# Attention and mixture of experts in one program: barriers between the stages removed, PSUM banks dealt anew, the gating moved into the last sequence, the attention's drain between the first experts

## The chip, the cores and the metric

The kernel runs on one core of one Trainium2 chip. The metric is the device time of a run in microseconds; lower is better. TensorE is called PE here, VectorE DVE, ScalarE ACT, GpSimd POOL and SyncE SP, as in the profile.

## What is computed

`x` has 16 sequences of 256 tokens of width 128, all in fp32. Four layers follow each other, each added to `x`:

```python
x = x + attn_a(layernorm(x))   # 16 heads of 8, q and k rms-normed, softmax, projection with bias
x = x + ffn(layernorm(x))      # 8 experts, the best two per token, and one shared expert
x = x + attn_b(layernorm(x))   # differential attention, 16 half-heads, rotary, projection
x = x + ffn(layernorm(x))      # the same weights again
```

In `ffn` every token gets softmax scores over 8 experts, keeps the best two, and the token times its score goes through `silu(xe @ w1[e]) * (xe @ w3[e]) @ w2[e]`; the shared expert takes the unscaled token.

## The kernel before, in words

All of `x` stays in SBUF. The attention layers (`attention_a` and `attention_b`) work on one sequence at a time, the feed-forward layers (`feed_forward`, called twice, with tags f and h) on chunks of 512 tokens (two pairs of tiles, i.e. two sequences), eight chunks in all. Each layer gives one `body` for each of PE, ACT, POOL and DVE, and a body emits the instructions of one step for its engine. All order is written out by hand: an engine runs its queue strictly in the order in which the bodies emit, and semaphores (class `Events`) tie the engines together.

A step of an attention is one sequence, cut into 16 slots h. `AT_A` and `AT_B` say at which slot each task runs, `STAGE_A` and `STAGE_B` for which sequence it does so: projection and normalisation run up to three or four sequences ahead of the scores, the output part one behind. In a step the PE makes the scores (L301 in A, L726 in B), ACT their exponentials (L414, L890), the PE the products with the values (L315, L756), which are copied out (L578 on DVE in A, L897 on ACT in B). One step later come the transposes of the output (L353, L820), the tokens' scaling on DVE (L545 and L548; L1053 to L1060), transposes (L360, L828), a copy (L439, L945), the output projection (L366, L834), the residual and the statistics for the next layer norm (L556 to L571, L1077 to L1097). B also has row maxima: the PE computes scores into two banks (L743) and DVE reduces them (L1023), eight times a sequence, two sequences ahead; and in its output part a difference, a square, a power and a product on POOL (L970 to L986), with a mean on DVE between them (L1066).

A step k of a feed-forward is one chunk, cut into nine slots e, one per expert and one for the shared one. At slot e the PE makes `up` of the next expert (six matmuls, L1211 to L1213, since each fp32 product is made from a high and a low part), the spread of the scores of an expert three ahead (L1207) and `down` of this one (L1241, eight matmuls by the profile). DVE scales (L1387), ACT makes the high part (L1320), POOL or DVE the low part (L1351, L1392), ACT the silu (L1305), DVE the product (L1403). Between them stands the gating of the next chunk: normalise (L1412), `x_turn` (L1258), copy (L1339), `logits` (L1264), `best` (L1421 to L1442), exponentials (L1328 on ACT for the first chunk, L1361 on POOL else), `gates` (L1448 to L1461), `s_turn` (L1271), copy (L1331). `FF` says at which slot each runs. Step -1 makes the gating and the first expert's `up` for chunk 0.

The program is one block for the setup and then four blocks: A with the step -1 of f behind it, f with the first two steps of B's preparation beside its last chunk (`BESIDE`), B with the step -1 of h, and h. Between blocks all engines meet at a barrier. `attention_steps` runs the 16 sequences (step 15 as a whole) and then step 16, the drain, slot by slot; at the slots of `SLOT_AT` it puts in the nine slots of the feed-forward's step -1:

```python
    slot = 0
    for h in range(HEADS):
        body(Step(None, 0, NSEQ), NSEQ, (h,))
        while slot <= E and SLOT_AT[slot] == h:
            following(Step(None, 0, -1), -1, (slot,))
            slot += 1
```

`feed_forward_steps` runs chunks 0 to 7 and a ninth step for the last residual. In PSUM (eight banks of 512 columns) A has scores in banks 0 to 3, the values' product in 4, the k and q transposes in 5, x and qkv in 6, the output part in 7; the feed-forward has its gating in 0, the spread in 1, H1 in 2 and 3, H3 in 4 and 5, Y in 6 and 7; B has x and qkv in 0, transposes in 1, maxima in 2 and 3, scores in 4 and 5, the values' product in 6 and the output part in 7.

Of the kernel before, what the change touches and what calls it, by code (L numbers as in the profile page):

```python
# [225 lines left out]
def attention_a(nc, ctx, g, psum):  # L226
# [401 lines left out]
    layer.ex_sb, layer.qkv_sb, layer.ot_sb, layer.rstd_sb = ex_sb, qkv_sb, ot_sb, rstd_sb  # L628
# [21 lines left out]
def attention_b(nc, ctx, g, psum, before):  # L650
# [26 lines left out]
    XB, QK, PV, OB = bank(0), bank(1), bank(6)[:, 0:SEQ], bank(7)  # L677
    M, S = psum[:, 1024:2048], psum[:, 2048:3072]
# [24 lines left out]
    def tensor(pe):  # L703
# [8 lines left out]
        def body(n, k, part=range(HEADS)):  # L712
# [34 lines left out]
            def values(m, km, q):  # L747

                if q == 0:
                    pe.wait_ge(v_sb.sem, v_sb.upto(m))  # L750
# [257 lines left out]
    def vector(dve):  # L1008

        def body(n, k, part=range(HEADS)):  # L1010
# [115 lines left out]
    layer.ex_sb, layer.qkv_sb, layer.qf_sb, layer.mx_sb, layer.ot_sb = ex_sb, qkv_sb, qf_sb, mx_sb, ot_sb  # L1126
    layer.rstd_sb = rstd_sb
# [6 lines left out]
SLOT_AT = (0, 2, 3, 6, 9, 9, 12, 14, 15)  # L1134
# [4 lines left out]
}  # L1139


def feed_forward(nc, ctx, g, tag, psum, before, out=None):
# [53 lines left out]
    def tensor(pe):  # L1196
        def body(n, k, part=range(E + 1)):
            run, gate = 0 <= k < NCH, 0 <= k + 1 < NCH

            def spread(m, km, e):  # L1200
# [73 lines left out]
            for e in part:  # L1274
# [5 lines left out]
                if gate and e == FF["x_turn"]:  # L1280
                    x_turn()
                if gate and e == FF["logits"]:
                    logits()
                if gate and e == FF["s_turn"]:
# [9 lines left out]
    def scalar(act):  # L1294
        def body(n, k, part=range(E + 1)):
            run, gate = 0 <= k < NCH, 0 <= k + 1 < NCH

# [24 lines left out]
            for e in part:  # L1322
                for m, km, next_e in ahead(n, k, e, 1):
                    silu(m, km, next_e)
                if k == -1 and e == FF["best"]:
# [3 lines left out]
                if gate and e == FF["st_sb"]:  # L1329
# [4 lines left out]
                if gate and e == FF["xt_sb"]:  # L1334
# [39 lines left out]
    def vector(dve):  # L1374
        def body(n, k, part=range(E + 1)):
            run, gate = 0 <= k < NCH, 0 <= k + 1 < NCH

# [105 lines left out]
            for e in part:  # L1483
# [11 lines left out]
                if gate and e == FF["best"]:  # L1495
                    best()
                if gate and e == FF["gates"]:
# [17 lines left out]
    layer.st_sb, layer.xe_sb, layer.h_sb, layer.rstd_sb = st_sb, xe_sb, h_sb, rstd_sb  # L1515
# [3 lines left out]
def attention_steps(eng, body, first, following):  # L1519
# [7 lines left out]
    for n in range(12, NSEQ):  # L1527
        body(Step(None, 0, n), n)
    slot = 0
    for h in range(HEADS):  # L1530
        body(Step(None, 0, NSEQ), NSEQ, (h,))
        while slot <= E and SLOT_AT[slot] == h:
            following(Step(None, 0, -1), -1, (slot,))
            slot += 1


def feed_forward_steps(eng, body, following=None):


    for n in (0, 1):  # L1540
        body(Step(None, 0, n), n)
# [10 lines left out]
    body(Step(None, 0, 8), 8)  # L1552

# [161 lines left out]
```

## Time and profile before

| | |
|---|---|
| Median of 3 runs | 1043.95 us (1042.01 to 1045.37) |
| The profiled execution: its time | 1042.84 us |
| its span, first to last instruction | 1041.0 us |
| PE busy | 885.7 us (85%), 7264 matmuls |
| DVE busy | 728.2 us (70%) |
| ACT busy | 579.5 us (56%) |
| POOL busy | 524.1 us (50%) |
| mean granted clock of the PE | 0.957 |

A busy time is the time in which an engine executes; what is idle is a wait or nothing to do. The page also cuts the span into 40 equal slices and gives the clock granted to the PE in each. Views of the trace give the same for any stretch, and the instructions of an engine in order of time, merged where the same line repeats, with the idle time before them and who ended it.

### The profile page before, as it was taken

The numbers are of one execution on the slowest core, as the hardware profiler recorded it, in microseconds if no ns is written. First come the engines' busy times: TensorE is split into PE (matmuls) and PEld (weight loads), VectorE is DVE, ScalarE is ACT, GpSimd is POOL, SyncE is SP. The second block draws the span as 40 slices with busy tenths as digits, with TensorE's granted clock in tenths as the row PEclk, the third lists the DMA queues.
The fourth block names the chain that finished last, engine by engine and source line by source line (L and its number), as shares of the span: only waits on it lengthen the run. The fifth ranks groups of instructions, "written<-read, shape, count | busy, mean of one in ns | idle before, by whom it ended". The sixth has DMA issues, their size and how long they took to land. (4 is left out here: it accounts for less than half of the span.)

```text
span 1041.0 us, 22276 instructions
## 1 busy us (share of the span) xinstructions
PE 885.7 (85%) x7264; PEld 628.1 (60%) x7264; DVE 728.2 (70%) x1970; ACT 579.5 (56%) x905; POOL 524.1 (50%) x606
## 2 busy tenths in 40 slices
PE   0498988887699999998788988888878499999998
PEld 0245555544478777886555555555544388888887
DVE  4357777775467777775568989899882477777775
ACT  1177777767344444443368888888875244444443
POOL 2556666674145455552425757575642354444441
PEclk9999999999699999999869999999996699999999
DMA  8000000000000000000000000000000000000000
GB/s 223 0 2 2 0 0 0 0 2 2 0 1 1 1 1 1 0 1 1 0 1 2 2 0 0 0 0 0 1 1 1 1 1 11 12 12 10 10 11 21
DMA packets 14591, 8.70 MB, mean 8 GB/s; under 512 B 1600, under 2 KB 14144, under 8 KB 14528
## 3 DMA queue, kind: packets, MB, share of 16 engines
q1 hardware_dynamic: 12944, 7.28, 2.5%
q8 instruction: 35, 0.57, 0.2%
q10 hardware_dynamic: 1584, 0.62, 0.2%
q14 instruction: 28, 0.23, 0.1%
HBM read 5.80 MB, written 2.10 MB: 8 GB/s over the span
## 5 line engine op out<-in xcount | busy, mean ns | idle before, releaser
L1320 ACT ACTIVATE f_xe_hi<-f_xe 128x512 fp32r<-128x512 f32 x128 | 80.9, 632 | 201.9 <-DVE f_xe L1387 201.9
L1023 DVE TENSOR_REDUCE s_qs<-psum 128x4 fp32r<-128x1024 f32 x128 | 156.4, 1222 | 43.7 <-PE psum L743 43.0
L1351 POOL TENSOR_TENSOR f_xe_lo<-f_xe,f_xe_hi 128x512 fp32r<-128x512 f32 x64 | 83.6, 1306 | 189.4 <-ACT f_xe_hi L1320 189.4
L1241 PEld LDWEIGHTS psum<-w,f_h 128*128 128x128 f32 x1152 | 148.5, 192 | 8.8
L1241 PE MATMUL psum<-w,f_h 128*128 128x128 f32 x1152 | 153.8, 277 | 0.0
L414 ACT ACTIVATE s_probs<-psum 128x1024 f32<-128x1024 f32 x128 | 125.5, 1024 | 31.8 <-PE psum L301 31.5
L890 ACT ACTIVATE s_probs<-psum 128x1024 f32<-128x1024 f32 x128 | 131.2, 1025 | 19.4 <-PE psum L726 17.8
L1211 PE MATMUL psum<-f_xe_hi,w_hi 128*128 128x512 f32 x288 | 127.7, 444 | 11.7 <-POOL f_xe_lo L1351 7.3
L1403 DVE TENSOR_TENSOR f_h<-psum,f_g 128x512 f32<-128x512 f32 x144 | 99.1, 688 | 49.0 <-ACT f_g L1305 35.5
L1213 PE MATMUL psum<-f_xe_lo,w_hi 128*128 128x512 f32 x288 | 114.9, 399 | 0.0
L1212 PE MATMUL psum<-f_xe_hi,w_lo 128*128 128x512 f32 x288 | 114.3, 397 | 0.0
L1387 DVE TENSOR_TENSOR f_xe<-psum,f_xt 128x512 f32<-128x512 f32 x128 | 87.3, 682 | 29.2 <-PE psum L1207 29.2
L1305 ACT ACTIVATE f_g<-psum 128x512 f32<-128x512 f32 x144 | 84.7, 588 | 23.9 <-PE psum L1213 23.6
L1361 POOL TENSOR_TENSOR f_p<-euler,f_sh 128x8 f32<-128x8 f32 x56 | 90.1, 1637 | 1.8
L726 PE MATMUL psum<-s_qt,s_kt 32*128 32x256 f32 x512 | 67.1, 339 | 22.1 <-DVE s_qs L1023 15.0
L726 PEld LDWEIGHTS psum<-s_qt,s_kt 32*128 32x128 f32 x512 | 40.7, 192 | 65.3 <-DVE s_qs L1023 30.4
L1392 DVE TENSOR_TENSOR f_xe_lo<-f_xe,f_xe_hi 128x512 fp32r<-128x512 f32 x64 | 44.3, 692 | 44.7 <-ACT f_xe_hi L1320 42.8
L743 PE MATMUL psum<-s_kt,s_qp 24*128 24x256 f32 x512 | 67.4, 342 | 9.0 <-PEq L1634 4.8
L756 PE MATMUL psum<-s_probs,s_v 128*32 128x256 f32 x1024 | 72.4, 402 | 0.0
L1211 PEld LDWEIGHTS psum<-f_xe_hi,w_hi 128*128 128x128 f32 x288 | 54.7, 190 | 28.9 <-issue 9.0
L315 PE MATMUL psum<-s_probs,s_v 128*32 128x256 f32 x1024 | 70.2, 393 | 0.0
L578 DVE COPY s_ot<-psum 128x256 f32<-128x256 f32 x64 | 26.8, 419 | 54.4 <-PE psum L315 54.3
(179 smaller groups left out, 1761.2 us busy)
## 6 DMA issues: line engine op xcount, KB each, us to landing
x<-in_x SPq DMA_DIRECT2D x4, 512.0 KB, 9.9
out<-x SPq DMA_DIRECT2D x8, 256.0 KB, 2.3
w<-in_w SPq DMA_DIRECT2D x3, 512.0 KB, 6.9
select_raw<-in_select SPq DMA_DIRECT2D x1, 512.0 KB, 5.0
rope_cos<-in_rope_cos SPq DMA_DIRECT2D x1, 256.0 KB, 3.6
rope_sin<-in_rope_sin SPq DMA_DIRECT2D x1, 256.0 KB, 4.5
wqkv_a<-in_Wqkv_aT ACTq DMA_DIRECT2D x1, 192.0 KB, 6.0
bqkv<-in_bqkv ACTq DMA_DIRECT2D x1, 192.0 KB, 7.1
```

The lines of the kernel that those rows point to most:

```text
L414: act.activation(dst, src, ACT.Exp).then_inc(ex_sb.sem, 1)
L726: ins = pe.matmul(S[:, o:o + SEQ], kt[r:r + 32, k % 2, q, c * P:(c + 1) * P], qt[r:r + 32, k % 2, q, :], start=True, stop=True)
L890: act.activation(probs[:, 2 * (i % 4):2 * (i % 4) + 2, :, :].rearrange("p j c s -> p (j c s)"), S, ACT.Exp).then_inc(ex_sb.sem, 1)
L1023: dve.tensor_reduce(o[:, r:r + 2, 2 * p:2 * p + 2, 24:25].bitcast(F32R), M.rearrange("p (r j s) -> p r j s", r=2, j=2), AX.X, ALU.max, neg ...
L1211: pe.matmul(dst, w_hi, x_hi, start=True, stop=False)
L1212: pe.matmul(dst, w_lo, x_hi, start=False, stop=False)
L1213: return pe.matmul(dst, w_hi, x_lo, start=False, stop=True)
L1241: ins = pe.matmul(Y[k % 2][:, t * P:(t + 1) * P], g.f_h[:, q, t * P:(t + 1) * P], g.w2[:, e, :], start=(e == 0 and t == 0), stop=(e == NE ...
L1305: act.activation(g.f_g[:, q, :], H1[q], ACT.Silu).then_inc(g_sb.sem, 1)
L1361: pool.tensor_tensor(g.f_p[:, i * w:(i + 1) * w], g.euler[:, 0:w], g.f_sh[:, i * w:(i + 1) * w], ALU.pow).then_inc(pw_sb.sem, 1)
L1387: dve.tensor_tensor(xe[:, e % 2, :], SB, xt[:, km % 2, :], ALU.mult).then_inc(xe_sb.sem, 1)
L1403: dve.tensor_tensor(g.f_h[:, q, :], H3[q], g.f_g[:, q, :], ALU.mult).then_inc(h_sb.sem, 1)
```

## The change

1. The four blocks become one: every engine runs `all_steps`, A, f, B and h in a row, with no barrier between them. SP's stores of the output stand in the same block.
2. The banks: B has scores in 2 and 3, maxima in 0 and 1, the values' product in 4, transposes in 5, x and qkv in 6, the output part in 7. The feed-forward has H1 in 0 and 1, H3 in 2 and 3, Y in 4 and 7, the spread in 5, the gating in 6. So gating and spread share their banks with the attention's preparation and not with its scores.
3. Step 15 of an attention is now emitted slot by slot too, and slots 0 to 7 of the feed-forward's step -1 stand in it, at the slots of `LEAD`. Within that step, `FF_LEAD` takes the place of `FF`.
4. In the drain (step 16) stand slot 8 of step -1 and all nine slots of chunk 0, at the slots of `TAIL_A` or `TAIL_B`; `feed_forward_steps` begins with chunk 1.
5. What the barriers assured is now assured by waits: for the last exponentials, for the last copy out of the values' bank, for the last residual, for the last transposes' use, and for the statistics of the layer before.

```diff
@@ attention_b, PE: values and o_turn
+                if km == 0 and q == 0:
+                    pe.wait_ge(before.x_sb.sem, before.x_sb.upto(Step(None, 0, NCH - 2)))
...
+                if km == 0 and c == 0:
+                    pe.wait_ge(before.x_sb.sem, before.x_sb.upto(Step(None, 0, NCH - 1)))
@@ attention_b, DVE: normalise
+                if km == 4:
+
+                    dve.wait_ge(before.rstd_sb.sem, before.rstd_sb.upto(Step(None, 0, NCH - 1)))
@@
-SLOT_AT = (0, 2, 3, 6, 9, 9, 12, 14, 15)
+LEAD = {1: (0,), 3: (1,), 4: (2,), 6: (3,), 8: (4,), 9: (5,), 13: (6,), 15: (7,)}
+TAIL_A = {1: ((-1, 8),), 4: ((0, 0),), 8: ((0, 1),), 11: ((0, 2),), 14: ((0, 3),),
+          15: ((0, 4), (0, 5), (0, 6), (0, 7), (0, 8))}
+TAIL_B = {1: ((-1, 8),), 4: ((0, 0),), 8: ((0, 1), (0, 2), (0, 3)), 12: ((0, 4),), 14: ((0, 5),),
+          15: ((0, 6), (0, 7), (0, 8))}
...
+FF_LEAD = {"x_turn": 0, "xt_sb": 1, "logits": 2, "best": 2, "exp": 4, "gates": 5, "s_turn": 6, "st_sb": 6}
@@ feed_forward
-    T, SB = psum[:, 0:512], psum[:, 512:1024]
-    H1 = [psum[:, 1024:1536], psum[:, 1536:2048]]
-    H3 = [psum[:, 2048:2560], psum[:, 2560:3072]]
-    Y = [psum[:, 3072:3584], psum[:, 3584:4096]]
...
+    T, SB = bank(6), bank(5)
+    H1, H3, Y = [bank(0), bank(1)], [bank(2), bank(3)], [bank(4), bank(7)]
@@ feed_forward, PE: spread, up, down, x_turn
+                    if km == 0:
+
+                        pe.wait_ge(before.turned.sem, before.turned.upto(last))
...
-                    pe.wait_ge(before.ot_sb.sem, before.ot_sb.upto(last))
+                    if not first:
+                        pe.wait_ge(before.mx_sb.sem, before.mx_sb.upto(last))
+                    pe.wait_ge(before.ex_sb.sem, before.ex_sb.upto(last))
...
+                if e == 0 and k == 0:
+
+                    pe.wait_ge(before.ot_sb.sem, before.ot_sb.upto(last))
+                if e == 0 and k == 1:
+
+                    pe.wait_ge(before.x_sb.sem, before.x_sb.upto(last))
...
-                    pe.wait_ge(before.ex_sb.sem, before.ex_sb.upto(last))
                     pe.wait_ge(before.qkv_sb.sem, before.qkv_sb.upto(last))
-                    if not first:
-                        pe.wait_ge(before.qf_sb.sem, before.qf_sb.upto(last))
-                        pe.wait_ge(before.mx_sb.sem, before.mx_sb.upto(last))
@@ feed_forward, DVE: normalise
+                if k == 1:
+
+                    dve.wait_ge(before.rstd_sb.sem, before.rstd_sb.upto(last))
@@ attention_steps
-    for n in range(12, NSEQ):
+    for n in range(12, NSEQ - 1):
         body(Step(None, 0, n), n)
-    slot = 0
+    for h in range(HEADS):
+        body(Step(None, 0, NSEQ - 1), NSEQ - 1, (h,))
+        for e in LEAD.get(h, ()):
+            following(Step(None, 0, -1), -1, (e,))
     for h in range(HEADS):
         body(Step(None, 0, NSEQ), NSEQ, (h,))
-        while slot <= E and SLOT_AT[slot] == h:
-            following(Step(None, 0, -1), -1, (slot,))
-            slot += 1
+        for k, e in tail.get(h, ()):
+            following(Step(None, 0, k), k, (e,))
@@ feed_forward_steps
-    for n in (0, 1):
-        body(Step(None, 0, n), n)
+    body(Step(None, 0, 1), 1)
@@
+def all_steps(eng, a, f, b, h):
+
+
+    attention_steps(eng, a, -3, f, TAIL_A)
+    feed_forward_steps(eng, f, b)
+    attention_steps(eng, b, -1, h, TAIL_B)
+    feed_forward_steps(eng, h)
```

## Rows read from the trace of the kernel before

**Rows 1.** Mean granted clock of the core; the page's clock in 40 slices (tenths).

```profile
core 0: 1041.0 us, clock 0.957
...
PEclk9999999999699999999869999999996699999999
```

**Rows 2.** Stretches: length, busy PE, PEld, DVE, ACT, POOL, granted clock, DMA.

```profile
263.70:287.60 23.90, 14.33 (x56) 9.15 (x55) 12.33 (x61) 5.97 (x10) 4.14 (x4) 0.57 0.00 0
271.30:273.40 2.10, 0.96 (x5) 0.56 (x4) 1.90 (x21) 0.23 (x1) 0.00 (x0) 0.50 0.00 0
289.80:316.10 26.30, 25.18 (x153) 21.70 (x152) 18.64 (x52) 11.31 (x20) 13.01 (x9) 1.00 0.00 1
484.60:488.00 3.40, 3.40 (x14) 2.96 (x13) 1.29 (x2) 0.90 (x2) 0.48 (x1) 0.55 0.00 0
508.50:511.90 3.40, 0.00 (x0) 0.00 (x0) 2.84 (x14) 0.00 (x0) 0.43 (x1) 0.95 0.00 0
778.20:781.60 3.40, 1.51 (x25) 0.86 (x18) 2.29 (x6) 1.86 (x4) 2.92 (x2) 0.94 0.00 0
786.60:804.60 18.00, 15.18 (x109) 7.97 (x109) 3.32 (x16) 9.89 (x14) 5.53 (x5) 0.59 0.00 1
804.60:830.80 26.20, 11.63 (x59) 7.95 (x58) 12.97 (x64) 6.66 (x11) 8.83 (x8) 0.66 0.00 1
```

**Rows 3.** Timeline of the PE, join 1: start, length, engine, line, operation [idle before].

```profile
253.82 0.51 PE L301 MATMUL psum<-s_qt,s_kt 32*128 32x256 f32 x8 [0.41 <-DVE s_qt L612]
...
266.56 1.09 PE L1258 MATMUL psum<-identity,f_xn 128*128 128x128 f32 x4 [2.82 <-DVE f_xn L1412]
267.57 1.93 PE L315 MATMUL psum<-s_probs,s_v 128*32 128x256 f32 x16
269.44 1.88 PE L1264 MATMUL psum<-gate,f_xt 128*128 128x8 f32 x8
...
282.97 0.63 PE L1212 MATMUL psum<-f_xe_hi,w_lo 128*128 128x512 f32 x1
283.40 0.63 PE L1213 MATMUL psum<-f_xe_lo,w_hi 128*128 128x512 f32 x1
...
288.22 0.39 PE L1213 MATMUL psum<-f_xe_lo,w_hi 128*128 128x512 f32 x1
288.45 0.39 PE L1211 MATMUL psum<-f_xe_hi,w_hi 128*128 128x512 f32 x1
...
289.80 1.06 PE L1241 MATMUL psum<-w,f_h 128*128 128x128 f32 x8
```

**Rows 4.** Timelines of ACT and DVE, join 1, the last exponentials and the gating.

```profile
262.15 1.94 ACT L414 ACTIVATE s_probs<-psum 128x1024 f32<-128x1024 f32 x2 [0.34 <-PE psum L301]
...
280.28 0.63 ACT L1320 ACTIVATE f_xe_hi<-f_xe 128x512 fp32r<-128x512 f32 x1 [1.61 <-DVE f_xe L1387]
...
265.19 1.11 DVE L1412 TENSOR_SCALAR f_xn<-x,mean,rstd 128x128 f32<-128x128 f32 x4
...
279.56 0.69 DVE L1387 TENSOR_TENSOR f_xe<-psum,f_xt 128x512 f32<-128x512 f32 x1 [2.69 <-PE psum L1207]
```

**Rows 5.** Timeline of all engines, join 2.

```profile
508.04 1.23 DVE L1023 TENSOR_REDUCE s_qs<-psum 128x4 fp32r<-128x1024 f32 x1 [3.43 <-PE psum L743]
...
512.84 0.80 PE L743 MATMUL psum<-s_kt,s_qp 24*128 24x256 f32 x4 [4.84 <-PEq L1634]
...
513.67 1.23 DVE L1023 TENSOR_REDUCE s_qs<-psum 128x4 fp32r<-128x1024 f32 x1 [2.21 <-PE psum L743]
```

**Rows 6.** Timelines of PE and POOL, join 3.

```profile
786.62 0.79 PE L726 MATMUL psum<-s_qt,s_kt 32*128 32x256 f32 x4
...
819.70 0.66 PE L828 MATMUL psum<-identity,s_an 128*128 128x128 f32 x2 [8.06 <-POOL s_an L986]
...
832.97 1.06 PE L1241 MATMUL psum<-w,f_h 128*128 128x128 f32 x8
...
815.94 2.91 POOL L980 TENSOR_TENSOR s_inv<-s_var,minus_half 128x16 f32<-128x16 f32 x1 [0.74 <-DVE s_var L1071]
```

More of the change, by code:

```diff
@@ L627, in attention_a @@
     layer.tensor, layer.scalar, layer.gpsimd, layer.vector = tensor, scalar, gpsimd, vector
-    layer.ex_sb, layer.qkv_sb, layer.ot_sb, layer.rstd_sb = ex_sb, qkv_sb, ot_sb, rstd_sb
+    layer.ex_sb, layer.qkv_sb, layer.ot_sb, layer.turned = ex_sb, qkv_sb, ot_sb, qp_sb
+    layer.x_sb, layer.rstd_sb = x_sb, rstd_sb
     return layer
@@ L1125, in attention_b @@
     layer.tensor, layer.scalar, layer.gpsimd, layer.vector = tensor, scalar, gpsimd, vector
-    layer.ex_sb, layer.qkv_sb, layer.qf_sb, layer.mx_sb, layer.ot_sb = ex_sb, qkv_sb, qf_sb, mx_sb, ot_sb
-    layer.rstd_sb = rstd_sb
+    layer.ex_sb, layer.qkv_sb, layer.turned, layer.mx_sb, layer.ot_sb = ex_sb, qkv_sb, qf_sb, mx_sb, ot_sb
+    layer.x_sb, layer.rstd_sb = x_sb, rstd_sb
     return layer
@@ L1279, in body @@
                         spread(m, km, next_e)
-                if gate and e == FF["x_turn"]:
+                if gate and e == AT["x_turn"]:
                     x_turn()
-                if gate and e == FF["logits"]:
+                if gate and e == AT["logits"]:
                     logits()
-                if gate and e == FF["s_turn"]:
+                if gate and e == AT["s_turn"]:
                     s_turn()
@@ L1296, in body @@
             run, gate = 0 <= k < NCH, 0 <= k + 1 < NCH
+            AT = FF_LEAD if k == -1 else FF
             def silu(m, km, e):
@@ L1324, in body @@
                     silu(m, km, next_e)
-                if k == -1 and e == FF["best"]:
+                if k == -1 and e == AT["exp"]:
                     act.wait_ge(sh_sb.sem, sh_sb.upto(n + 1))
                     act.activation(g.f_p[:], g.f_sh[:], ACT.Exp).then_inc(pw_sb.sem, PIECES)
-                if gate and e == FF["st_sb"]:
+                if gate and e == AT["st_sb"]:
                     act.wait_ge(st_mm.sem, st_mm.upto(n + 1))
@@ L1333, in body @@
                     high(m, km, next_e)
-                if gate and e == FF["xt_sb"]:
+                if gate and e == AT["xt_sb"]:
                     act.wait_ge(xt_mm.sem, xt_mm.upto(n + 1))
@@ L1376, in body @@
             run, gate = 0 <= k < NCH, 0 <= k + 1 < NCH
+            AT = FF_LEAD if k == -1 else FF
             def scale(m, km, e):
@@ L1494, in body @@
                         scale(m, km, next_e)
-                if gate and e == FF["best"]:
+                if gate and e == AT["best"]:
                     best()
-                if gate and e == FF["gates"]:
+                if gate and e == AT["gates"]:
                     gates()
@@ L1514, in feed_forward, with attention_steps @@
     layer.tensor, layer.scalar, layer.gpsimd, layer.vector, layer.sync = tensor, scalar, gpsimd, vector, sync
-    layer.st_sb, layer.xe_sb, layer.h_sb, layer.rstd_sb = st_sb, xe_sb, h_sb, rstd_sb
+    layer.st_sb, layer.xe_sb, layer.h_sb, layer.x_sb, layer.rstd_sb = st_sb, xe_sb, h_sb, x_sb, rstd_sb
     return layer
-def attention_steps(eng, body, first, following):
+def attention_steps(eng, body, first, following, tail):
     for n in range(first, 2):
@@ L1613, in program, with _ @@
         h = feed_forward(nc, ctx, g, "h", psum, b, out)
-        for layer, following, first in ((a, f, -3), (b, h, -1)):
-            with nc.Block() as block:
-                @block.tensor
-                def _(pe):
-                    attention_steps(pe, layer.tensor(pe), first, following.tensor(pe))
-                @block.scalar
-                def _(act):
-                    attention_steps(act, layer.scalar(act), first, following.scalar(act))
-                @block.gpsimd
-                def _(pool):
-                    attention_steps(pool, layer.gpsimd(pool), first, following.gpsimd(pool))
-                @block.vector
-                def _(dve):
-                    attention_steps(dve, layer.vector(dve), first, following.vector(dve))
-            with nc.Block() as block:
-                after = b if layer is a else None
-                @block.tensor
-                def _(pe):
-                    feed_forward_steps(pe, following.tensor(pe), after and after.tensor(pe))
-                @block.scalar
-                def _(act):
-                    feed_forward_steps(act, following.scalar(act), after and after.scalar(act))
-                @block.gpsimd
-                def _(pool):
-                    feed_forward_steps(pool, following.gpsimd(pool), after and after.gpsimd(pool))
-                @block.vector
-                def _(dve):
-                    feed_forward_steps(dve, following.vector(dve), after and after.vector(dve))
-                if following is h:
-                    @block.sync
-                    def _(sp):
-                        h.sync(sp)
+        with nc.Block() as block:
+            @block.tensor
+            def _(pe):
+                all_steps(pe, a.tensor(pe), f.tensor(pe), b.tensor(pe), h.tensor(pe))
+            @block.scalar
+            def _(act):
+                all_steps(act, a.scalar(act), f.scalar(act), b.scalar(act), h.scalar(act))
+            @block.gpsimd
+            def _(pool):
+                all_steps(pool, a.gpsimd(pool), f.gpsimd(pool), b.gpsimd(pool), h.gpsimd(pool))
+            @block.vector
+            def _(dve):
+                all_steps(dve, a.vector(dve), f.vector(dve), b.vector(dve), h.vector(dve))
+            @block.sync
+            def _(sp):
+                h.sync(sp)
 def constants():
```

7 lines of the change are left out of this document (5 added, 2 removed).

## The prediction, made before the change was run

> **What bounds the kernel now.** I read the mean clock and the page's table of slices first. Of 40 slices of 26 us, the granted clock is below nine tenths in slices 11, 20, 21, 31 and 32, so around 270, 520 and 800 us; a mean of 0.957 makes 2 x 0.043 x 1041 = 90 us at half clock [rows 1]. In between, each stage runs at its own pace, as a feed-forward chunk does: 26.3 us, of which the PE is busy 25.2 [rows 2]. The change touches nothing there. So I asked for the busy time by stretch. The reader should see three joins. From 263.7 to 287.6 the PE is busy 14.3 of 23.9 us, with a granted clock of 0.57. From 804.6 to 830.8 it is busy 11.6 of 26.2 us, at 0.66. From 508.5 to 511.9 it does nothing at all [rows 2]. Then I read the PE's own timeline through each join, because the order of its queue is what the change rewrites.
>
> **Join 1 before (attention A to feed-forward).** The last sequence begins with its scores at 253.82. After its exponentials comes one long chain: DVE normalises, PE transposes (266.56) and makes the logits (269.44), DVE finds the two best and the gates, the PE transposes and spreads them, then scale, high part, low part, and expert 0's up matmuls about 283. The barrier follows, and the first down projection starts at 289.80 [rows 3, 4]. From first scores to first down: 289.80 - 253.82 = 36.0 us.
>
> **Join 1 after.** The gating slots move to the last sequence. I add their steps to it with the durations they have today, the PE's brought to full clock: successive up matmuls start 0.43 us apart at the low clock (282.97 to 283.40) and 0.23 apart at the full one (288.22 to 288.45), a ratio of 1.85 [rows 3]. So four transposes take 1.09 / 1.85 = 0.6, logits 1.0, values 1.05, one spread 0.3 and an expert's six up matmuls 1.4.
> - In the first quarter the x transposes stand behind a DVE copy (about 0.4, an estimate: half the width of the 0.69 of scale) and the normalising (1.11 [rows 4]). The PE has the values' 1.05 to do meanwhile and then the transposes: it loses 1.5 to 1.7 us, I take 1.7.
> - Logits, and 2 us of DVE for the two best [rows 2] ahead of the copy that the next values need: another 0.5. The cover is a quarter's round, in which ACT's two exponentials (1.94) follow the scores (0.5) and the PE has little over half of that time to fill; without this slack the 2 us would be paid whole.
> - At the fourteenth slot ACT waits in its queue for the gates' transposes, its own copy of them (as wide as the high part), a spread, scale, and does the high part: 0.6 + 0.6 + 0.3 + 0.69 + 0.63 and four handovers of some 0.1 = 3.3 us [rows 4], and the last exponentials are queued behind it.
> The last values can therefore start 5.5 us later than now: they could start at 264.1 (end of the last exponentials, 262.15 + 1.94 [rows 4]), which is 10.3 after the first scores, so now 15.8. Behind them stand values 1.05, up of expert 0 (1.4), a spread, the first of the output transposes (0.6), up of expert 1 (1.4), a spread and the next chunk's transposes (0.6), 5.7 in all and some 0.4 of handovers: first down at 21.9. Saved: 36.0 - 21.9 = 14.1 us. The barrier is inside it.
> Given back: the rest of the drain (four transposes, two transposes and four 128-column matmuls, 0.6 + 0.4 + 0.6 = 1.6, I take 1.7) now lies in the first chunk, where the PE is the bound with 25.2 busy of 26.3 [rows 2], so it is paid in full. Its DVE part (two tokens steps, residual, statistics, some 2.6 us, an estimate) hides in the 7.7 us that DVE idles in a chunk, and its one ACT copy likewise: nothing. And the PE is thin between the s transposes and the last values, so I expect one short spell of low clock. The nearest row is the one at 484.6: 3.4 us at 0.55 with the PE busy throughout, and then back [rows 2]. Each us of dense work at low clock loses 1 - 1/1.85 = 0.46, so one or two such spells lose 1.6 to 3.1 us; I take 2.5. **Join 1: 14.1 - 1.7 - 2.5 = 9.9 us.** Bounds: 12.4 with no low clock, 5 if the DVE's two best and the waits of the in-order queues cost twice what I gave them.
>
> **Join 2 (feed-forward to attention B).** Only the barrier goes. Today DVE does one reduction of the maxima (508.04 to 509.27) and then the last residual with its statistics; before the second reduction, at 513.67, it has stood 2.21 us for the PE's next maxima, which the barrier held back by 4.84 [rows 5]. The PE needs no more than the end of the first reduction to issue them, so the second starts when the statistics end: **2.2 us** saved. What is late next is the same DVE. Bounds: 1, if POOL's work is what is waited for; 5, if the clock also stayed up, since the eight alternations of PE and DVE behind it would take 0.8 - 0.8/1.85 = 0.37 us less each [rows 5]. I take the low end, because the PE still idles through most of 508 to 512, and after such a stretch the maxima ran at the low clock.
>
> **Join 3 before (attention B to feed-forward).** From the last sequence's first scores, 786.62, to the first down, 832.97: 46.35 us. The sequence itself takes 18.0 at a granted clock of 0.59. In the drain, DVE's tokens, POOL's difference, square, 2.91 us of pow and the product hold the PE for 8.06 us, and the gating's transposes stand behind them in the PE's queue [rows 2, 6].
> **Join 3 after.** The same summation as above, twice. At full clock: eight rounds of scores (0.5) and one exponential (0.97), 11.8 us, in which values and drain hide; 1.5 at the first quarter, 2.8 for logits and the PE work that no longer fits beside the exponentials, 1.6 for gates' transposes and the first spread, 3.3 for ACT's slot 13: last values at 21.0. Then values, up 0, both output transposes and about 1.4 us of waiting for DVE's tokens between and before them, up 1, two spreads, transposes: 7.7, first down at 28.7. At low clock throughout: the 18.0 us of today plus 5.4 of gating on the PE (1.09 + 1.88 + 1.09 + 2 x 0.63 [rows 3]) and 2.5 of ACT's stall that nothing covers: last values at 25.9, and the 6.3 us of PE work behind them at 1.85, less what overlaps with the tokens, makes the first down at 37. Today the clock falls about 781.4, before anything that moves: the PE was busy 1.51 of 3.4 us there, and the sequence behind it has a mean of 0.59 [rows 2]. The added work is dense, so the clock should rise sooner; I take 31.5, a third of the way. Saved: 46.35 - 31.5 = 14.9. Given back: transposes and projection in the chunk 1.0, and 2.4 for what the drain does to in-order queues: DVE's mean of squares waits for POOL's square, which stands behind POOL's low part of expert 3, and POOL's 2.91 us of pow [rows 6] stands ahead of the low part of expert 4 and of the pow that the next gating needs. **Join 3: 11.5 us.** Bounds: 16.5 (28.7, all hidden but the 1.0) and 6 (37, 3.4 given back).
>
> The Trainium skill, on the page TensorE: Matmul & The Clock Gate (Part 1, "What's actually happening"), says that "the default state is throttled, and activity releases the throttle". By that alone a filled join has the full clock, and the sum would be the upper bounds. The trace agrees where the experts run at 288 at full clock, but about 781.4 it falls amid a running sequence.
>
> The moved banks cost nothing: in every stage the PE, ACT and DVE touch as many banks as before, and the new waits (on x_sb, rstd_sb, turned, mx_sb) ask for things done one or more experts earlier. The barrier behind the setup stays. Exponentials and silu stay apart, so the number of table loads does too. No DMA moves; SP only waits in its own queue from the start.
>
> **Sum.** 9.9 + 2.2 + 11.5 = 23.6 us. The profiled execution took 1042.84 us (span 1041.0, 1.8 around it) and is 1.1 below the median of 1043.95. 1043.95 - 23.6 = **1020.4 us**.
>
> **Rivals.**
> - The clock stays up (the skill's rule). Saved 12.4 + 5 + 16.5 = 34: 1010 us, or a little less. For it: the 90 us at half clock all lie near the joins. Against: the fall at 781.4, and the idle stretch that remains at 508. Chance 0.13.
> - The gating is not hidden in the last sequences. Each scores needs the exponentials before it, and ACT and DVE run in order, so every wait of the gating's chain lands in a loop that has no slack. If the last sequences grow by 9 to 10 us instead of 5.5 and 4: saved 5 + 1 + 5 = 11, 1033 us. For it: the gating's chain from 266.56 to 283 is 16 us long today, mostly latency. Chance 0.12.
> - Slower: the clock stays low through the first chunk of experts at both feed-forward joins. A chunk of 26.3 us at 1.85 takes 48.6: +22.3 each, 44.6 - 23.6 = +21, 1065 us. It decides from about 58 us of additional low clock under dense matmuls (each costs 0.46 us; 26.7 are needed to get beyond 0.3%). Against: at both joins the clock returned just as the experts became dense. Chance 0.04.
> - The change does not do what it says: a new wait (the last exponentials before the first up, the last ot copy before the first down) comes so late that the order on paper is not the order in time, and only the barriers are saved, within 3 us of before. Chance 0.03.
>
> Forecast 0.68. A measurement of this kernel tells about 0.3% (3.1 us) from no change. Faster: forecast and the first two rivals, 0.93; same 0.03; slower 0.04. The range goes from 1009 (the upper bounds) to 1032 (the lower bounds: 5 + 1 + 6), which leaves out parts of the first two rivals and the last two.
>
> **What would show it.** First down after the last sequence's first scores: 22 to 25 us at join 1 and 29 to 34 at join 3, against 36.0 and 46.35. No PE wait on a semaphore of the barrier. The last A sequence about 15 us. The PE's 8.06 us of idle for POOL's product gone. Low clock down from 90 us to 50 to 65. DVE's second reduction at join 2 within 0.2 us of the statistics' end. I am wrong if the last sequences grow by over 8 us, if the first chunks take over 31 us, or if the stages between the joins change their pace.

## The result and the profile after

The changed kernel takes **1021.29 us** (median of 4 runs, 1018.06 to 1023.82) where the kernel before, run beside it, took 1044.66: a ratio of 0.9772 [0.9745, 0.98]. The forecast was 1020.4. The profiled execution after is the longest of the four, 1023.82 us; against the 1042.84 of the profiled one before that is 19.0 less, and all differences between traces below are differences of these two executions.

The mean clock, and the page's clock in 40 slices (tenths), as [rows 1]:

```profile
core 0: 1022.0 us, clock 0.965
...
PEclk9999999999799999998859999999997899999999
```

Low clock adds up to some 72 us in the span (2 x 0.035 x 1022.0), against some 89 before. The three dips are still there; the first and third are shallower, the middle one is not. By stretch, as [rows 2] (length, busy PE, PEld, DVE, ACT, POOL, granted clock, DMA):

```profile
259.30:269.50 10.20, 10.20 (x80) 6.06 (x82) 4.19 (x30) 5.08 (x7) 0.00 (x0) 0.53 0.01 2
280.40:308.94 28.54, 27.33 (x169) 23.46 (x168) 21.91 (x65) 11.93 (x22) 13.63 (x10) 1.00 0.00 1
505.10:535.80 30.70, 25.38 (x134) 16.01 (x138) 16.56 (x19) 13.91 (x22) 8.25 (x9) 0.51 0.00 1
779.04:797.30 18.26, 15.26 (x118) 8.52 (x118) 7.37 (x46) 10.08 (x15) 4.88 (x4) 0.65 0.01 2
797.30:810.30 13.00, 9.45 (x54) 6.32 (x53) 7.05 (x17) 6.15 (x9) 3.25 (x3) 0.84 0.00 1
810.31:840.50 30.19, 26.77 (x166) 22.96 (x165) 21.49 (x73) 11.70 (x21) 19.07 (x15) 1.00 0.00 1
```

The second and last rows are the first chunks of the two feed-forwards, which now hold the attention's drain: 28.54 and 30.19 us against 27.07 and 27.09 before, from the first down projection to the chunk's residual. At the third join, the 46.35 us from the last sequence's first scores to the first down are now 18.26 + 13.00.

**Join 1.** The PE's timeline from the last sequence's first scores, as [rows 3] (start, length, engine, line, operation, idle before):

```profile
255.45 0.51 PE L301 MATMUL psum<-s_qt,s_kt 32*128 32x256 f32 x8 [0.41 <-DVE s_qt L612]
...
258.58 0.96 PE L1280 MATMUL psum<-identity,f_xn 128*128 128x128 f32 x4 [1.62 <-issue]
...
261.05 1.88 PE L1286 MATMUL psum<-gate,f_xt 128*128 128x8 f32 x8
...
270.42 0.66 PE L1293 MATMUL psum<-identity,f_ss 128*128 128x128 f32 x4
271.81 0.47 PE L1225 MATMUL psum<-f_st,select 128*128 128x512 f32 x1 [0.73 <-issue]
...
274.64 1.07 PE L315 MATMUL psum<-s_probs,s_v 128*32 128x256 f32 x16 [1.07 <-ACT s_probs L414]
275.64 0.51 PE L1229 MATMUL psum<-f_xe_hi,w_hi 128*128 128x512 f32 x1
...
280.43 1.06 PE L1267 MATMUL psum<-w,f_h 128*128 128x128 f32 x8
```

The whole gating (transposes L1280, logits L1286, gates' transposes L1293, first spread L1225) now lies between the scores and values of the last sequence, and the ups follow the last values at once. First scores to first down is 280.43 - 255.45 = 25.0 us, before 36.0. ACT's timeline shows what the sequence pays, with ACT's copy of the gates (L1354) and the high part of expert 0 (L1343) ahead of the last exponentials:

```profile
269.55 1.02 ACT L414 ACTIVATE s_probs<-psum 128x1024 f32<-128x1024 f32 x1
271.12 0.60 ACT L1354 ACTIVATE f_st<-psum 128x512 fp32r<-128x512 f32 x1 [0.54 <-PE psum L1293]
273.04 0.63 ACT L1343 ACTIVATE f_xe_hi<-f_xe 128x512 fp32r<-128x512 f32 x1 [1.33 <-DVE f_xe L1411]
273.58 1.01 ACT L414 ACTIVATE s_probs<-psum 128x1024 f32<-128x1024 f32 x1
```

The stall from 270.57 (269.55 + 1.02) to 273.58 is 3.0 us; the working had 3.3.

**Join 2.** DVE's reductions, and what lies between them, as [rows 5]:

```profile
500.96 1.23 DVE L1028 TENSOR_REDUCE s_qs<-psum 128x4 fp32r<-128x1024 f32 x1 [3.44 <-PE psum L744]
502.10 0.68 DVE L1492 TENSOR_TENSOR x<-psum,x 128x512 f32<-128x512 f32 x1
...
504.23 0.16 DVE L1507 COPY mean<-s_mv 128x4 f32<-128x4 f32 x1
504.30 1.22 DVE L1028 TENSOR_REDUCE s_qs<-psum 128x4 fp32r<-128x1024 f32 x1
...
507.11 1.22 DVE L1028 TENSOR_REDUCE s_qs<-psum 128x4 fp32r<-128x1024 f32 x1
```

The second reduction starts as the statistics end (504.30, no idle time ahead of it), 3.34 us after the first; before it was 5.63 us after it. That is the forecast 2.2, to 0.1. Yet from the last residual of f to the first of B the traces read 56.50 us before and 56.72 after: the gain is gone by then. The row 505.10:535.80 above says where. Low clock lasts 30.7 us here, 27.3 before; it ends 30.9 us after the second reduction begins (at 535.2), before it ended 25.2 us after it (at 538.9). An estimate with the prediction's 0.46 us per us of low clock makes the 5.7 us more worth 2.6 us, which is what was lost: 2.3 + 0.2.

**Join 3.** POOL, DVE and PE in the first chunk, as [rows 6]:

```profile
812.00 1.29 POOL L1374 TENSOR_TENSOR f_xe_lo<-f_xe,f_xe_hi 128x512 fp32r<-128x512 f32 x1 [8.49 <-ACT f_xe_hi L1343]
...
814.05 0.61 POOL L981 TENSOR_TENSOR s_sq<-s_a 128x256 f32<-128x256 f32 x1
814.70 0.42 DVE L1074 TENSOR_REDUCE s_ms<-s_sq 128x16 f32<-128x256 f32 x1 [3.45 <-POOL s_sq L981]
815.41 2.91 POOL L985 TENSOR_TENSOR s_inv<-s_var,minus_half 128x16 f32<-128x16 f32 x1 [0.74 <-DVE s_var L1079]
...
818.97 1.27 POOL L1374 TENSOR_TENSOR f_xe_lo<-f_xe,f_xe_hi 128x512 fp32r<-128x512 f32 x1
...
820.29 0.50 PE L1229 MATMUL psum<-f_xe_hi,w_hi 128*128 128x512 f32 x1 [2.30 <-POOL f_xe_lo L1374]
```

The 8.06 us in which the PE stood for POOL's pow and product are gone; the pow still takes 2.91 us, but under the experts. In their place are two smaller waits, both in order: DVE stands 3.45 us for a square that POOL takes up only behind its low part, and the PE stands 2.30 us for the low part queued behind the pow and the product. First scores (779.04) to first down is 31.3 us.

Set side by side, the differences after minus before grow like this over the trace: +1.6 us before join 1 (it has a spell of low clock at 217.8 that the trace before has not), -9.5 across join 1 and its chunk, +0.8 over the rest of f, +0.2 across join 2, -12.7 from there through join 3 and its chunk, +0.6 behind it: -19.0.

### The profile page after: what moved, and what is told of

Read it like the earlier page. It is cut to its first block, busy times and chain, and to the rows that moved or that the text cites. A ratio compares the mean times of both kernels' runs of the same rounds, so it can differ in the third digit from the quotient of the medians.

```text
span 1022.0 us, 22245 instructions
## 1 busy us (share of the span) xinstructions
PE 883.0 (86%) x7264; PEld 625.6 (61%) x7264; DVE 728.8 (71%) x1970; ACT 579.1 (57%) x905; POOL 523.8 (51%) x606
## 4 chain that ended last, share of the span: by engine, by line
PE 21%; issue 13%; DVE 11%; POOL 7%; ACT 2%; DVEq 0%; POOLq 0%; ACTq 0%
DVE s_qs L1028 6%; PE psum L759 5%; PE psum L727 4%; POOL f_xe_lo L1374 3%; POOL f_p L1384 3%; PE psum L1267 2%; PE psum L709 2%; PE psum L1229 1%; PE psum L814 1%; DVE f_xe L1411 1%; PE psum L825 1%; PE psum L1231 1%; PE psum L1230 1%; PE psum L744 1%; ACT f_xe_hi L1343 1%
## 5 line engine op out<-in xcount | busy, mean ns | idle before, releaser
L1343 ACT ACTIVATE f_xe_hi<-f_xe 128x512 fp32r<-128x512 f32 x128 | 80.9, 632 | 202.8 <-DVE f_xe L1411 202.8
L895 ACT ACTIVATE s_probs<-psum 128x1024 f32<-128x1024 f32 x128 | 131.2, 1025 | 19.2 <-PE psum L727 17.6
L744 PE MATMUL psum<-s_kt,s_qp 24*128 24x256 f32 x512 | 67.8, 344 | 8.0 <-DVE s_qs L1028 7.1
L759 PE MATMUL psum<-s_probs,s_v 128*32 128x256 f32 x1024 | 73.5, 407 | 1.1 <-ACT s_probs L895 1.1
L315 PE MATMUL psum<-s_probs,s_v 128*32 128x256 f32 x1024 | 72.0, 401 | 1.1 <-ACT s_probs L414 1.1
```

Source lines behind the costliest of these rows:

```text
L759: ins = pe.matmul(PV[32 * j:32 * j + 32, :], v1[:, km % 2, c, h // 2, :], probs[:, h % 8, c, :], start=(c == 0), stop=(c == 1))
L895: act.activation(probs[:, 2 * (i % 4):2 * (i % 4) + 2, :, :].rearrange("p j c s -> p (j c s)"), S, ACT.Exp).then_inc(ex_sb.sem, 1)
```

## One part at a time

The theory was the forecast's: the time comes from the two filled joins, little from the barriers, nothing from the banks. Its rivals were that the barriers or the banks carry it, and that moving the gating alone would do. Four kernels form a staircase; all shared a chip, and the kernel before took 1041.88 us on it. The ratios are those of all runs of a kernel together, so they need not equal the quotient of the medians.

**The banks and their waits alone**: the orders and the four blocks of before, on the code of after.

```diff
-LEAD = {1: (0,), 3: (1,), 4: (2,), 6: (3,), 8: (4,), 9: (5,), 13: (6,), 15: (7,)}
+LEAD = {}
...
+TAIL_A = {0: ((-1, 0),), 2: ((-1, 1),), 3: ((-1, 2),), 6: ((-1, 3),), 9: ((-1, 4), (-1, 5)), 12: ((-1, 6),),
+          14: ((-1, 7),), 15: ((-1, 8),)}
...
+FF_LEAD = {"x_turn": 0, "xt_sb": 0, "logits": 1, "best": 1, "exp": 1, "gates": 5, "s_turn": 6, "st_sb": 6}
...
-                all_steps(pe, a.tensor(pe), f.tensor(pe), b.tensor(pe), h.tensor(pe))
+                attention_steps(pe, a.tensor(pe), -3, f.tensor(pe), TAIL_A)
...
```

> The kernel after with the old order and all four barriers back: what is left of the change is the banks and the new waits. Theory (moved work): the same as the kernel before, within 2 us. Rival (banks): if the scores' banks 0 to 3 shared with H1 and H3 help or hurt PE, ACT and DVE in the stages between the joins, the time is off by more than 3 us and the pace of a chunk (26.3 us) or of a sequence of B (16.9 us) moves.

Measured: 1044.65 us, 1.0008 [0.9986, 1.003]. The PE's timeline at join 3 of this kernel:

```profile
819.08 0.66 PE L833 MATMUL psum<-identity,s_an 128*128 128x128 f32 x2 [8.07 <-POOL s_an L991]
...
830.24 0.47 PE L1229 MATMUL psum<-f_xe_hi,w_hi 128*128 128x512 f32 x1 [1.94 <-PEq L1689]
832.37 1.06 PE L1267 MATMUL psum<-w,f_h 128*128 128x128 f32 x8
```

The two marks of before are back: 8.07 us for POOL's product, and 1.94 us for the PE's own sequencer, which is the barrier. The banks and the new waits cost nothing and bring nothing that the time shows. One stage does differ: from the first residual of h to the last it is 177.9 us in this trace and in every other one with the new banks, 177.35 in the one before. What that half us is was not separated.

This kernel also shows how far a single trace of one order can be trusted: it has the order and the barriers of the kernel before and nearly its span (1040.9 us and 1041.0), but join 1 reads 37.2 us and join 3 43.4, where that one reads 36.0 and 46.35. The low clock falls differently in the two.

**Without barriers**: the same old order in one block.

```diff
+LEAD = {}
...
+          14: ((-1, 7),), 15: ((-1, 8),) + tuple((0, e) for e in range(9))}
...
+FF_LEAD = {"x_turn": 0, "xt_sb": 0, "logits": 1, "best": 1, "exp": 1, "gates": 5, "s_turn": 6, "st_sb": 6}
```

> One block, no barriers, but the gating's step -1 in the drain and chunk 0 behind it, in the old order. Theory (moved work): the barrier held the PE for 1.9 us at each feed-forward join and DVE for 2.2 us at join 2, so 3 to 6 us faster than before, 1039 to 1042. Rival (barriers): if the barriers with their drains and the restart of five queues are what cost, most of the 23 us is here already: 1021 to 1028.

Measured: 1037.79 us, 0.9958 [0.9941, 0.9976], a little under the expected range; the three barriers between the four blocks are worth 0.4%, 4.4 us. First scores to first down is 33.7 us at join 1 and 44.7 at join 3, and join 2 is 55.2. With the barriers the two traces have 36.0 and 37.2, 46.35 and 43.4, and 56.5 twice, so the readings show some 1.3 us at join 2 and 2.3 to 3.4 at join 1, and leave open what the barrier at join 3 cost.

**The gating moved, the drain not**: `LEAD` and `FF_LEAD` as in the change, chunk 0 behind the whole drain.

```diff
-TAIL_A = {1: ((-1, 8),), 4: ((0, 0),), 8: ((0, 1),), 11: ((0, 2),), 14: ((0, 3),),
-          15: ((0, 4), (0, 5), (0, 6), (0, 7), (0, 8))}
+TAIL_A = {1: ((-1, 8),), 15: tuple((0, e) for e in range(9))}
...
+TAIL_B = {1: ((-1, 8),), 15: tuple((0, e) for e in range(9))}
```

> The gating in the last sequence as in the kernel after, but the drain runs through alone, with expert 0's up in it, and chunk 0 stands behind it. Theory (moved work, both halves needed): the drain is a chain of some 8 us in A and 13 us in B, in which nothing else has work, so the first down comes only 3 to 5 us earlier than before at each join: 1032 to 1038. Rival (the gating alone): the 16 us of the gating's chain were all that cost, and the drain would hide anyway: 1021 to 1026.

Measured: 1031.28 us, 0.9896 [0.9865, 0.9926], just under the expected range. Join 1 reads 29.8 and join 3 40.2 us. The chunk behind join 3 takes 27.09 us again, so the 3.1 us that it grew by in the changed kernel come from the drain inside it. Moving the gating alone leaves about half of the gain at join 3 untaken, since the PE still stands for POOL in the drain, as its timeline shows:

```profile
814.81 0.66 PE L833 MATMUL psum<-identity,s_an 128*128 128x128 f32 x2 [7.02 <-POOL s_an L991]
```

**Join 3 as in the change, join 1 in the old order**:

```diff
-TAIL_A = {1: ((-1, 8),), 4: ((0, 0),), 8: ((0, 1),), 11: ((0, 2),), 14: ((0, 3),),
-          15: ((0, 4), (0, 5), (0, 6), (0, 7), (0, 8))}
+TAIL_A = {0: ((-1, 0),), 2: ((-1, 1),), 3: ((-1, 2),), 6: ((-1, 3),), 9: ((-1, 4), (-1, 5)), 12: ((-1, 6),),
+          14: ((-1, 7),), 15: ((-1, 8),) + tuple((0, e) for e in range(9))}
...
+FF_OLD = {"x_turn": 0, "xt_sb": 0, "logits": 1, "best": 1, "exp": 1, "gates": 5, "s_turn": 6, "st_sb": 6}
...
-            AT = FF_LEAD if k == -1 else FF
+            AT = (FF_OLD if first else FF_LEAD) if k == -1 else FF
...
-        for e in LEAD.get(h, ()):
+        for e in (LEAD.get(h, ()) if first == -1 else ()):
```

> Old order at join 1, new order at join 3, no barriers. Theory (the joins add up): what is saved is join 3 (some 12 us), join 2's barrier (2) and join 1's barrier (2): 1027 to 1031, 7 to 9 us slower than the kernel after. Rival (the clock couples them, or one join does it all): within 3 us of the kernel after, or above 1036.

Measured: 1026.92 us, 0.9851 [0.9826, 0.9876]. Join 3 reads 31.4 us as in the changed kernel, join 1 34.3 as without barriers. The new order at join 3 is thus worth 1037.79 - 1026.92 = 10.9 us. What is left to the changed kernel is join 1. It did not run on this chip: by its first comparison it is 0.9851 to 0.9772, 0.0079 x 1042 = 8 us, and by the repeat below (0.9717) it is 14, each with an interval of some 3 us, so this pair does not pin it.

The staircase 1.0008, 0.9958, 0.9896 (or 0.9851), and then 0.9772 or 0.9717 refutes the rivals: neither banks, barriers nor the gating alone carry it.

## The waits and the low clock that are left

The first four kernels of this section shared a chip, where the kernel before took 1044.91 us. Where matmuls are added, nobody reads their result, and nothing is left out of the computation.

**The drain ahead of the experts in POOL's queue.** If the in-order waits in the chunk of join 3 come from the order in POOL's and DVE's queues, one number moves them: expert slot 0 of the chunk behind slot 6 of the drain rather than slot 4.

```diff
-TAIL_B = {1: ((-1, 8),), 4: ((0, 0),), 8: ((0, 1), (0, 2), (0, 3)), 12: ((0, 4),), 14: ((0, 5),),
+TAIL_B = {1: ((-1, 8),), 6: ((0, 0),), 8: ((0, 1), (0, 2), (0, 3)), 12: ((0, 4),), 14: ((0, 5),),
```

> The kernel after with slot 0 of chunk 0 in B's drain moved from slot 4 to slot 6, so that POOL's difference and square stand ahead of the low part of expert 3. Theory (in-order queues): DVE's 3.45 us wait for the square and the PE's 2.3 us wait for expert 4's low part go, and the stretch from the first down of h to its first residual shrinks from 30.2 to 27 to 28 us: 2 to 3 us faster than the kernel after. Rival (PE bound): the chunk is held by the PE's added drain work, and it is the same within 1 us.

Measured: 1015.94 us, 0.9722 [0.9698, 0.9746]. The first row is DVE's timeline, the second is the PE's, in the chunk:

```profile
811.06 0.42 DVE L1074 TENSOR_REDUCE s_ms<-s_sq 128x16 f32<-128x256 f32 x1
```

```profile
817.82 0.51 PE L1229 MATMUL psum<-f_xe_hi,w_hi 128*128 128x512 f32 x1 [0.83 <-POOL f_xe_lo L1374]
```

DVE's 3.45 us wait is gone, the PE's 2.30 is 0.83, and the chunk takes 28.04 us instead of 30.19: 2.1 of the 3.1 us were the in-order waits.

**A busy PE at join 2.** If low clock is what eats the gain of join 2, and the PE's idle time is what brings it, then unread matmuls in that idle time should raise it and pay; if DVE's alternation with the PE is the bound at either clock, nothing changes.

```diff
+                    pe.matmul(dst, g.w1_hi[:, 0, :], g.w1_hi[:, 1:5, :], start=True, stop=True)
...
+                if k == -1 and h % 2 == 0:
+                    keep_busy(bank(3), 8 if h == 0 else 2)
```

> The kernel after plus 22 matmuls whose result nobody reads, at full clock 0.23 us each: eight behind the second maxima of join 2, two behind each of the other seven. Theory (clock at join 2): removing the barrier gained 2.2 us on DVE and lost it to 30 us of half clock; with the PE kept busy the granted clock stays near 1.0 from 505 to 536, low clock falls from 72 to about 42 us, and 3 to 5 us are gained. Rival (DVE and chain bound): the clock rises but the time does not change by more than 1 us, or the added matmuls stand in the way and it is slower.

Measured: 1014.22 us, 0.9717 [0.9693, 0.974], mean clock 0.983. The PE's timeline (L744 makes the maxima, L846 is unread) and the stretch that answers to 505.10:535.80 above:

```profile
497.44 0.50 PE L744 MATMUL psum<-s_kt,s_qp 24*128 24x256 f32 x4 [1.32 <-DVE s_qs L1035]
497.87 3.41 PE L846 MATMUL psum<-w_hi 128*128 128x512 f32 x8
...
503.76 0.50 PE L744 MATMUL psum<-s_kt,s_qp 24*128 24x256 f32 x4
```

```profile
499.20:502.60 3.40, 3.40 (x14) 2.46 (x14) 2.02 (x7) 0.55 (x1) 2.40 (x3) 0.63 0.00 0
502.60:519.70 17.10, 13.43 (x88) 9.02 (x88) 11.59 (x13) 8.05 (x14) 5.84 (x6) 0.97 0.00 1
```

Four matmuls of the maxima take 0.50 us each time down to 513.76, where those after 505 take 0.79 in the changed kernel, and the 30.7 us of low clock have shrunk to two spells of 3.4. From residual to residual join 2 is 51.64 us instead of 56.72: **5.1 us**. Against the 56.50 of the kernel before it is 4.9, and the prediction's upper bound, with the clock up, was 5. The Trainium skill says on the page TensorE: Matmul & The Clock Gate (Part 1, "What's actually happening") that activity releases the throttle. These rows agree: the only thing added is 22 matmuls.

**A busy PE in the last sequences.** Such matmuls where the PE idles in the last sequence of A and the last two of B.

```diff
+                if k == 15 and h in (1, 3):
...
+                    for _ in range(6 if h == 1 else 1):
+                        pe.matmul(QK, g.w1_hi[:, 0, :], g.w1_hi[:, 1:5, :], start=True, stop=True)
...
+                if k == 14 and h in (8, 10, 12):
+                    keep_busy(XB, 2)
+                if k == 15 and h % 2 == 0:
...
+                    keep_busy(bank(0), 2)
```

> The kernel after plus matmuls whose result nobody reads in the last sequences: seven in A (six before the first transposes of the gating), and two behind each scores in B's last sequence and in three slots before it. Theory (clock): the low spells at 259 to 269, 775 to 778 and 785 to 799 go, first down after first scores falls from 25.0 to 22 to 23 at join 1 and from 31.3 to 28 to 29 at join 3, in all 4 to 6 us faster than the kernel after. Rival (ACT's chain): exponentials, copies and handovers set the pace of the last sequences and not the PE, so the same within 1.5 us.

Measured: 1015.86 us, 0.9722 [0.9699, 0.9744], mean clock 0.974. Low clock is some 52 us in all; join 1 reads 22.4 and join 3 29.6 us, against 25.0 and 31.3. The PE's first scores and last values of the last A sequence:

```profile
256.24 0.50 PE L301 MATMUL psum<-s_qt,s_kt 32*128 32x256 f32 x8 [0.42 <-DVE s_qt L618]
...
271.82 1.66 PE L315 MATMUL psum<-s_probs,s_v 128*32 128x256 f32 x16 [1.07 <-ACT s_probs L420]
```

The scores and transposes between them ran at their short lengths (0.51 us, and 0.60 to 0.66), and the last values start 15.6 us after the first scores, where the changed kernel has 274.64 - 255.45 = 19.2. The 1.07 us of waiting for the last exponentials are there in both. The joins of one more kernel warn against reading this to the us: the one with a busy PE at join 2 has nothing added in the last sequences and reads 22.7 and 29.6 us in its trace, with spells of low clock of 3.4 us at join 1 and 10.2 at 781.6. What sets the additions apart is that no low clock at all is left between 541.8 and 801.2, where the changed kernel has 3.4 us of it at 774.1 and 13.7 at 784.4.

**ACT's stall later.** Slot 6 of the gating moved from slot 13 of the last sequence to its end, behind the last exponentials.

```diff
-LEAD = {1: (0,), 3: (1,), 4: (2,), 6: (3,), 8: (4,), 9: (5,), 13: (6,), 15: (7,)}
+LEAD = {1: (0,), 3: (1,), 4: (2,), 6: (3,), 8: (4,), 9: (5,), 15: (6, 7)}
```

> The kernel after with slots 6 and 7 of the gating both at slot 15 of the last sequence, so that the last exponentials no longer stand behind ACT's copy, the first spread, scale and high part. If ACT's 3.3 us stall were what is paid, first down after first scores would fall by 2 to 3 us at both joins, 4 to 6 us faster in all. Theory (the gating's own chain is the bound there): the values start a little earlier, but expert 0's up waits for its low part as long as before: the same within 1.5 us.

Measured: 1016.74 us, 0.973 [0.9701, 0.976]. Join 3 reads 31.4, as before the edit. Join 1 reads 20.6 us, 4.4 less than in the changed kernel, which was not expected. Its stretch to the last values and the one behind them, and the PE's row of the last values, now without a wait:

```profile
254.90:269.60 14.70, 10.93 (x128) 6.71 (x128) 9.70 (x57) 9.99 (x13) 1.39 (x2) 1.00 0.01 2
269.60:275.50 5.90, 5.30 (x40) 3.95 (x40) 5.18 (x11) 3.68 (x6) 2.57 (x2) 1.00 0.01 3
```

```profile
269.63 1.07 PE L315 MATMUL psum<-s_probs,s_v 128*32 128x256 f32 x16
```

The clock stays at full speed throughout. But in the changed kernel it fell at 258.7, three us after the first scores, when both kernels had issued the same instructions; the edit lies behind that. So the fall is a matter of the execution, and most of the 4.4 us is what it costs. The other traces with the unchanged order at join 1 say the same: 10.2 us of low clock and 25.0 us of join twice (the changed kernel and the one with the drain order), 6.8 and 23.4 in the repeat, 3.4 and 22.7 with the busy PE at join 2. The last pair below bears this out.

The totals of these four kernels, 1014 to 1017 us, can't be told from each other nor from the changed kernel's own spread; it is the stretches that separate them.

**Together.** The changed kernel once more, and the three edits (drain order, both groups of unread matmuls), then with the fourth, on one chip where the kernel before took 1046.18 us.

> The kernel after, unchanged, beside the others: the base for what they gain on the same chip. The same as in the first measurement, 0.975 to 0.980 of before, about 1021 us. Its low spells of the clock differ by execution, so single profiles of it are 1018 to 1024.

> The drain order of f1 and the unread matmuls of f2 and f3 together. Theory (three separate losses that the change left): they add up, 2 us of in-order waits, 5 us of half clock at join 2 and 4 us in the two last sequences: 1009 to 1012 us, low clock under 20 us. Rival (one chain, the gains overlap): no better than the best of them alone, 1014.

> As g2 and both last gating slots at slot 15. f4 showed 20.6 instead of 25.0 us from first scores to first down at join 1, of which 2.5 may be its luckier clock, and nothing at join 3 (31.4). With the clock held in both, what is left is the order: if ACT's stall is paid, 1 to 2 us faster than g2 at join 1 (20.6 against 22.4); if it was all clock, the same as g2.

Measured: the changed kernel 1017.34 us, 0.9717 [0.9696, 0.9737]; with the three edits **1007.37 us**, 0.9643 [0.9618, 0.9669]; with all four 1009.25 us, 0.9639 [0.9618, 0.966]. The repeat is outside the 0.975 to 0.980 that were expected, and the one with three is below the expected 1009 to 1012. The mean clock and the slices of the one with three:

```profile
core 0: 1005.2 us, clock 0.993
...
PEclk9999999999999999999999999999999999999999
```

Some 14 us of low clock are left. Against the changed kernel on the same chip it is 1007.37 / 1017.34 = 0.990, 10.0 us. The fourth edit adds nothing: join 1 reads 22.2 us with three and 21.9 with four, so its own worth is some 0.3 us. Join 2 reads 51.8 us with three and 54.6 with four, by the same unread matmuls: in the second trace 10.2 us of low clock are left there, a spell of 3.4 at 505.8 and one of 6.8 at 519.4. So the added matmuls do not assure a high clock.

## Why the prediction was right

- **Join 1 (9.9 net).** Right: 9.5 net. The sum had 21.9 at full clock plus 2.5 for the clock, 24.4; the changed kernel shows 25.0, and the execution in which the clock stayed up 20.6 with the later spread. The drain in the chunk was forecast at 1.7 and is 28.54 - 27.07 = 1.5. Its parts: the working put the last values at 15.8 us after the first scores with the clock up, and the kernel with unread matmuls there shows 15.6. What stands behind them was put at 6.1 us and takes 280.43 - 274.64 = 5.8. ACT's stall was 3.0 for 3.3. The term that was mis-sized is the clock: one spell of 10.2 us in place of one or two of 3.4, at a cost of 19.2 - 15.6 = 3.6 us in place of 2.5. The sign "the last A sequence about 15 us" is missed for it in this execution (19.2 us to the last values, 17.7 in the repeat).
- **Join 2 (2.2).** The mechanism was right, and the gain on DVE is 2.3. The step that failed is that it is kept: "I take the low end, because the PE still idles" took the clock as the same as before, and it stayed low 3.4 us longer, or 5.7 counted from the second reduction. From residual to residual nothing is left (56.50 and 56.72, and 56.70 in the repeat). Without barriers in the old order 1.3 us of it were kept. What is late next was named right, DVE; that it would be late at a price set by the PE's clock, as the busy PE shows (51.64), was the other end of the range.
- **Join 3 (11.5).** Right: 31.3 us for the forecast 31.5, a chunk that grows by 3.1 for the forecast 3.4, and 10.9 us when measured alone. The 46.35 that it started from was one execution's (43.4 in another of the same order), so the 12.0 net that the two traces give is closer to the forecast than it could be relied on to be. The last values start 801.14 - 779.04 = 22.1 us after the first scores, between the 21.0 and the 25.9 of the two clocks. Both waits that the working named are in the trace, at 3.45 and 2.30 us.
- **Banks and waits (0).** Right: 1.0008.
- **Low clock.** Forecast 50 to 65 us, found some 72. The largest part is join 2 with 30.7, more than the 27.3 of before.
- **Rivals.** The clock did not stay up of itself. With unread matmuls it nearly does (0.993), and with the drain's order mended too the kernel takes 1007.4 where that rival had 1010. The gating not hidden (1033) does not hold: with the clock up the last values come 15.6 - 10.3 = 5.3 us later than they could before, as the forecast's 5.5 had it, not 9 to 10. At the clock that the changed kernel has it is 8.9, though (7.4 in the repeat), so what was named as a sign of being wrong (growth by over 8 us) did appear, and it was the clock. The slower rival does not hold: both first chunks run at a granted clock of 1.00. The repeat has one spell of 3.4 us in the first chunk of h, which then takes 31.8 us, over the 31 that the prediction also named as such a sign; it is one spell and not a chunk at low clock.
- **The difference of the profiled pair**, 19.0 us, is less than the 23.4 between the medians. Part is the forecast's own: 9.9 + 2.2 + 11.5 = 23.6 lost the 2.2 of join 2 in the trace, and the rest of f came 0.8 longer. Part is that the profiled execution is the longest of four, with a clock of 0.965 where the shortest, 1018.06 us, has 0.971. So 1020.4 was met a little better than its terms deserve: that the medians agree to 1 us is in part luck.

What stays open: why the repeat on another chip gives 0.9717 [0.9696, 0.9737] where the first comparison gave 0.9772 [0.9745, 0.98]. The two do not overlap. The changed kernel's part is its clock: the medians are 1021.29 us at 0.9675 and 1017.34 at 0.973, and 5.5 times the 0.71 us per 0.001 of the last section is 3.9. Why the clock was lower in the first comparison, and why the kernel before went the other way (1044.66 and 1046.18), was not pursued.

## What to carry to other kernels

Where two stages meet, follow the PE's queue from the first instruction of the last full step to the first of the next stage's dense work: that distance, summed from today's durations with each in-order queue counted, gave both joins to within 1 us, once an allowance for low clock was added. A gain of some us on another engine can be eaten whole by low clock, so ask of every join how long the PE idles there; 22 unread matmuls in that idle time, on operands in place and a free bank, brought 5.1 us at one join in one trace, 4.9 in another and 2.1 in a third; the three barriers together cost 4.4. When an interleaved drain has a slow operation on POOL, put the drain's small POOL operations ahead of the chunk's, not behind.

## What the runs showed of the hardware that was not expected

- **The time of one and the same kernel follows its granted clock.** Of 22 runs of the kernel before on one chip the shortest took 1039.40 us at a mean clock of 0.964 and the longest 1049.07 at 0.951; a line through all has a slope of 0.65 us per 0.001. The changed kernel repeated: 1015.33 at 0.975 to 1022.27 at 0.966, 0.71 per 0.001. So the spread between runs is for the most part low clock that falls differently, and 0.5% between two kernels says little until the clocks are compared.
- **The clock falls or holds at the same instructions from one execution to the next**: at 258.7 in the changed kernel for 10.2 us, for 6.8 and 3.4 us in two other traces, and not at all in the one with the later spread, all with the same instructions up to there and the same 1.6 us of idle PE just before (1.62 in the row 258.58).
- **It can stay low under a PE that the trace calls busy.** From 505.1 to 535.8 the PE was busy 25.38 of 30.70 us and the clock 0.51. With 22 more matmuls ahead of and among the same work, most of it ran at 0.97 (502.60 to 519.70 of that kernel). What in them does it was not separated.
